# Graph network on one Trainium2 core: the prologue's round counts and scatters four edge tiles in place of three

## The reference

```python
feat_all = einsum('ni,rhid->rnhd', inputs, conv_weights)
e = leaky_relu(sum(feat_all[edge_type, edge_src] * attn_l[edge_type], -1)
             + sum(feat_all[edge_type, edge_dst] * attn_r[edge_type], -1))
alpha = softmax of e over the edges of one destination
h = segment_sum(alpha[..., None] * feat_all[edge_type, edge_src], edge_dst)
...
out = segment_sum(msg, dst)          # layers 2 to 4: msg = h[src], with other factors
```

## Time and profile before

| what | us |
|---|---|
| median of 3 runs | 3265.38 (3260.52 to 3266.35) |
| the profiled execution, its span | 3494.0 |
| DVE, POOL, PE busy in it | 1869.1, 1013.3, 2934.6 |
| mean granted clock of PE | 0.904 of 2.4 GHz |

### The profile page before, as it was taken

The page is one execution under the profiler, slowest core; times in us unless marked ns, Lnnn a source line. Parts: engine busy times, 40 slices in busy tenths (PEclk is TensorE's granted clock), DMA queues, the critical chain, the costliest instruction groups (busy, mean ns, idle before and its releaser), DMA issues.

```text
span 3494.0 us, 48240 instructions
## 1 busy us (share of the span) xinstructions
PE 2934.6 (84%) x15020; PEld 1947.6 (56%) x15084; DVE 1869.1 (53%) x5320; ACT 1260.7 (36%) x3665; POOL 1013.3 (29%) x1048
## 2 busy tenths in 40 slices
PE   2799936888888888889268799989999999999998
PEld 2444416777777777778142444445555555545545
DVE  6578745666666665556250543334555555532334
ACT  1122235666666666668020220004444444420000
POOL 2144465666666666665710000000000000000000
PEclk6699968898999899999559699999999999999999
DMA  8966643222222222221128243330000000022232
GB/s 250 363 180 194 183 125 86 70 73 74 71 74 71 73 74 72 74 66 28 31 71 301 82 119 103 101 118 6 3 6 6 6 3 6 23 76 79 78 101 80
DMA packets 245032, 314.35 MB, mean 90 GB/s; under 512 B 121467, under 2 KB 168484, under 8 KB 240740
## 3 DMA queue, kind: packets, MB, share of 16 engines
q1 hardware_dynamic: 191412, 175.79, 17.8%
q0 software_dynamic: 49104, 104.11, 10.2%
q10 hardware_dynamic: 4320, 31.95, 2.3%
HBM read 234.14 MB, written 77.59 MB: 89 GB/s over the span
## 4 chain that ended last, share of the span: by engine, by line
PE 57%; DVE 15%; issue 11%; ACT 7%; another core or an unknown queue 4%; DVEq 3%; DMA 3%; SPq 0%; ACTq 0%
PE PS L1153 15%; PE PS L998 14%; PE PS L964 7%; PE PS L939 5%; PE PS L977 5%; PE PS L822 4%; ACT BG L653 3%; DMA BG<-a_d 3%; DVE BG L1703 2%; DVEq L1582 2%; DVE OHB L1430 1%; ACT SL L736 1%; DVE AL L1790 1%; DVE SUMS L1411 1%
## 5 line engine op out<-in xcount | busy, mean ns | idle before, releaser
L1567 DVE TENSOR_TENSOR SUMS<-SUMS,PS 128x640 f32 x500 | 409.2, 818 | 374.2 <-PE PS L939 220.7
L532 POOL DMA_INDIRECT BG<-feat_d,IDXST x500 | 485.9, 972 | 337.9 <-PE PS L939 157.4
L523 POOL DMA_INDIRECT a_d<-VAL,IDXS x499 | 492.3, 987 | 314.3 <-DVE VAL L1424 133.2
L1153 PE MATMUL PS<-BG,SL 128*128 128x512 f32 (+1 forms) x1440 | 539.1, 530 | 12.0 <-ACT SL L736 12.0
L653 ACT ACTIVATE BG<-BG,SL 128x64 f32<-128x64 f32 x2000 | 513.4, 336 | 0.0
L1153 PEld LDWEIGHTS PS<-BG,SL 128*128 128x128 f32 x1440 | 277.0, 195 | 251.7 <-issue 222.4
L564 POOL MEMSET BG<- 128x7680 f32 x1 | 6.5, 6501 | 1327.3 <-DVE MV L1834 1327.3
L964 PE MATMUL PS<-W1A,X 65*128 65x256 f32 x1000 | 295.2, 421 | 81.8 <-ACT X L627 60.4
L939 PE MATMUL PS<-OHB,BG 128*128 128x128 f32 x2000 | 357.2, 305 | 0.2
L977 PE MATMUL PS<-OHB,X 128*128 128x128 f32 x2000 | 337.5, 295 | 23.1 <-issue 22.6
L977 PEld LDWEIGHTS PS<-OHB,X 128*128 128x128 f32 x2000 | 306.7, 208 | 40.0 <-issue 25.1
(11 more groups left out here) (298 smaller groups left out, 4093.0 us busy)
## 6 DMA issues: line engine op xcount, KB each, us to landing
BG<-a_d SPq DMA_DIRECT2D x171, 256.0 KB, 4.2
AL<-a_d SPq DMA_DIRECT2D x137, 256.0 KB, 2.6
a_d<-BG POOLq DMA_DIRECT2D x30, 1088.0 KB, 40.2
feat_d<-SUMS ACTq DMA_DIRECT2D x30, 1040.0 KB
BG<-rel_d SPq DMA_DIRECT2D x100, 160.0 KB
X<-in_edge_attr_dram SPq DMA_DIRECT2D x124, 128.0 KB
SUMS<-a_d SPq DMA_DIRECT2D x52, 256.0 KB, 2.6
SL<-key_d SPq DMA_DIRECT2D x50, 192.0 KB
```

The source lines that it names most:

```text
L523: pool.indirect_dma_start(a_d.rearrange("n (w o) -> (n w) o", o=1), bass.IndirectOffsetOnAxis(ap=IDXS[:, t:t + 1], axis=0), VAL[:, t:t + 1 ...
L532: pool.indirect_dma_start(RING[:, t // NB % 3, t % NB, :], None, feat_d.rearrange("n (r d) -> (n r) d", r=R), bass.IndirectOffsetOnAxis(ap ...
L1153: last = pe.matmul(PS[:, to + q, 0:width], lhs[:, i, c, :], w[:, c, q * width:(q + 1) * width], start=(c == 0), stop=(c == kc - 1))
L1567: add = tt(a, a, SUM_AT[n % 3].rearrange("p (a n) -> p a n", a=5), ALU.add)
```

## The change

CT, the number of edge tiles that a prologue round counts and scatters, is 4 in place of 3.

```diff
-        CT = 3
+        CT = 4
         SOON = CT * IT
```

## The result

The changed kernel takes 3210.85 us (median of 4 runs, 3207.44 to 3212.16), the kernel before 3264.56 (4 runs, 3260.52 to 3266.35): ratio 0.9835, 95% interval 0.9821 to 0.9849. The direction was right and so was the cost; the gain was mis-sized.

A forecast was written before the change was run, and what follows sets the result against it. It took DVE to pace the prologue's rounds and POOL's tail of scatters to gate the a_d loads. Prologue plus 13 against a gain of 35 or 51 gave -22 or -38; it took -28, 3237 us, range 3216 to 3256.

The forecast's parts named there:

- Prologue, DVE: plus 13 us: Prologue rounds: 50 more counts on DVE at 0.27 us lengthen the rounds by 13 us, bounds 0 and 17.
- Prologue, POOL: 0: Prologue: 50 more scatters, four a round, fit into POOL's room and add 0, at most 1.3 us.
- the cover: End of prologue: the first gather's wait for the table's last store hides the last round's fourth scatter, by 1.1 us.
- Edge loop: 0: Edge loop: 50 fewer counts on DVE and turnings on PE gain 0, bound 13 us.
- a pace of 22 tiles: Edge loop: 22 tiles in 50 us with and without counts, so neither count nor turning paces a tile.
- rival 3: Edge loop: PE or DVE paces the counted tiles, so it gains 13 us more, 3224 us; chance 0.10.
- After the loop, POOL: minus 35 to 51 us: Tail: scatters after the last gather shrink from 142 to 92, gaining 35 to 51 us, bounds 0 and 63.
- from 105 to 71: 35 us: Home stage running freely: the gate after the last addition moves from 105 us of scatters to Y's 71, gaining 35.
- -22 and -38: Whole kernel: prologue's 13 us less a gain of 35 (home stage undisturbed) or 51 (as profiled); -28 taken between.
- the crawl: Home stage as first profiled: home tiles slowed until some 12 us after the last scatter, with long waits naming no engine.
- Rival 1: Home stage: Y, not the scatters, already opens the a_d loads; only the prologue's 13 us remain, 3278 us; chance 0.10.
- Rival 2: Prologue: PE's 93% is the pace and hides the added counts; 3230 us, or 3214 with the full 51; chance 0.10.

The follow-up runs named there:

- experiment 1: Changed kernel, counting four tiles a round but scattering only 150 tiles in the prologue, so 142 scatters stay in the tail: 3279.51 us, ratio 1.0038 to the kernel before.
- second profile of before: The unchanged kernel profiled once more, nothing edited: span 3265.8 us, in agreement with its timed runs.
- experiment 4: Kernel before without its last 50 scatters and without the 50 counts and turnings beside tiles 300 to 349: 3199.85 us, ratio 0.9799.
- the long execution: First profile of the unchanged kernel, from which the prediction's rows come: span 3494.0 us, against timed runs of 3265.38.
- experiment 10: Changed kernel with tile 498 scattered from its 6 real rows and the loop's scatters starting 14 gathers later, 7 moved to the tail: 3191.77 us, ratio 0.9785.
- experiment 3: Kernel before with the last 50 scatters left out, tile 498 among them: 3193.7 us, ratio 0.9786.
- experiment 2: Kernel before with a fourth count into scratch on DVE in each of 50 prologue rounds, nothing else: 3269.23 us, ratio 1.0016.
- experiment 6: Kernel before with tile 498 (6 real edges, 122 pads) scattered first in the tail in place of last: 3254.16 us, ratio 0.9968.
- experiment 9: Changed kernel with tile 498 scattered from its 6 real rows alone, in its old place as the last: 3203.37 us, ratio 0.9819.
- experiment 7: Changed kernel with tile 498 scattered first in the tail in place of last: 3219.07 us, ratio 0.9856.
- experiment 5: Kernel before with the 50 scatters of tiles 448 to 497 left out, tile 498 kept as the last: 3202.85 us, ratio 0.9815.
- experiment 8: Kernel before with tile 498 scattered from its 6 real rows alone, in its old place as the last: 3248.71 us, ratio 0.9958.

## Why the prediction was half right

*Prologue, DVE: plus 13 us.* Right: the last cast came 11.7 us (experiment 1) and 13.3 us (after) later, the first gather 12.7 us, or 12.0 as a mean over profiles, and the runs of experiment 1 lost 12. The casts stand about 6.5 us apart after, as the forecast said.

*Prologue, POOL: 0.* Off by 0.7 us, within the 1.3 that the forecast allowed if the cover were gone. It is gone: the first gather now follows the last scatter directly (the rows above). That 13 us for the whole prologue came out so exactly is partly luck: the wait for the table's store hides 1.4 us of the longer rounds. The sentence on a DVE copy that locks POOL out (Trainium skill, SBUF — State Buffer, section SBUF: two separate sides) named a danger for this place. No lengthening by the fourth scatter shows: the 192 scatters between 130 and 465 us after take 971 ns each, against 978 in the second profile of before. Where scatters do take longer beside DVE is in the tail, in the 12 of 1.28 us and more above. The prediction had no term for them. That it is the lock that lengthens them was not tried.

*Edge loop: 0.* Right, by experiments 1 and 4. But the argument from the earlier trace rows rested on a pace of 22 tiles that only the long execution has. The reason given against rival 3, POOL's 1.9 us for a gather and half a scatter, is the one that experiment 10 bears out.

*After the loop, POOL: minus 35 to 51 us.* This is the step that failed. It let the gate move "from 105 to 71: 35 us" (its own numbers give 34). By the profiles it moved from 142.0 to 73.8: 68.2 us, more even than the bound of 63. Three parts were missing on the before side, 37 us together. First, 94 scatters follow the last addition and not 83: 14 us. The forecast had POOL "held back by the tiles, one scatter each" up to the last tile; in the second profile of before it is not held, it issues 48 scatters at its own pitch in the 64.1 us from the last gather to the last addition. The long execution took 99.4 us from the one to the other, and 59 of its 142 scatters fell into them. Second, the last scatter lands 18.5 us behind its end on POOL, which the forecast put at nothing, because in the earlier trace rows the landing was hidden behind Y. Third, the slow scatters beside DVE, and a few single ones, stretch the 94 from 118.8 to 123.6 us: 5 us. After, the scatters end at 55.3, and with the landing at 73.8, only 6.8 us behind Y and 3 us behind the 71 that the forecast had for Y. So the 50 scatters were worth their full 63 us and 5 more, where the forecast thought 28 us of them covered by Y.

*The sum.* With the second profile the same steps give 13 - 68 = -55, against -53.7 measured. The choice between -22 and -38 was made between two readings of an execution that matches neither. The doubt was there ("the profiled execution is slower somewhere"), and its answer went the wrong way: the tail without the crawl was taken to be worth less, from an 83 that itself came out of the crawl.

*The crawl.* The second profile of before has no such waits in the home stage (30 statistics L1610 from 1449.19 to 1492.29, 1.49 us apart). It was a matter of that one execution. What slowed it stays open. A queue of the recording that was full and held its producer up, which the Trainium skill (NOTIFIC — the notification-queue block, section Overflow: three behaviours, one of which stalls the engine) describes as possible, is not shown by any run here; the second profile of the same program and the profiles of all the other kernels did not have the crawl.

*Rivals.* Rival 1 (the gain does not come) falls with experiment 3. Rival 2 (the prologue hides the counts) falls with experiment 1; experiment 2 missed its 12.5 us, but it too moved the last cast by 8 of the 9 us that it added on DVE. Rival 3 falls with experiments 1 and 4. None of them held the missing 26 us. Of the signs that the forecast named, the casts and the first gather came as said; the pace of 22 tiles, the 33 scatters behind the last addition (44) and the load 105 us behind it (73.8) did not.

## What to carry to other kernels

Before a gate is priced, ask when each thing it waits for has landed, not when its engine has issued it; a wait that the profile hides behind a later one has a length too, and it appears as soon as the later one goes. If a profiled execution is 7% longer than the runs, take a second one before counting anything in it, counts of instructions between two events included. Pads that all write to one dummy address are not free: leave them out of the transfer, and do not move such a transfer to where other engines are busy.

## What the runs showed of the hardware

- An indirect DMA of 128 two-byte values, 122 of them to one address, lands 19.2 us after its start on POOL; with its 6 real ones alone 1.91 us, and one of 128 real edges within 2.2 us (experiment 6). By these numbers one of the 122 costs about (19.24 - 1.91) / 122 = 0.14 us, an estimate. Only this one tile was measured, so that the writes go one behind the other is inferred.
- While it lands, an instruction packet of another queue takes 3.1 to 3.4 us (five profiles), without the 122 writes 0.4 us in the same place (experiment 9).
- 11 to 19 us after such a scatter was issued beside the busy loop, PE, ACT and DVE began to stand, for 12 to 19 us, with no releaser in the profile (experiments 6 and 7). Whether it would do the same to the home stage can't be read here: after and in experiment 5, Y was ready 12 to 13 us after the scatter was issued.
- Beside DVE's L1589 (24 times 125 x 640, 0.80 us each) 11 scatters took 1.28 to 1.29 us in place of 0.96 and one before them 1.23 to 1.57, in all five profiles looked at that have scatters left there (second profile of before, experiments 1, 2, 6 and 8). What lengthens them was not tried.
- Before a count of 128 x 128 on DVE whose output column the round sets, DVE idled 0.27 us (experiment 1), before one with a fixed output column 0.18 us (experiment 2). One case of each; the cause was not tried.
